# A gated cross-attention and mixture-of-experts kernel on one core: value weights, turns and one GpSimd pass moved, and the last expert's scatter written without adding

## The reference

```python
x = x + tanh(g_xattn) * slot_attention(layernorm(x), ctx)       # x: 4 x 1024 x 256, ctx: 4 x 64 x 256
x = x + tanh(g_ffn) * moe(layernorm(x))

def slot_attention(slots, P):                  # three iterations over the same weights
    k, v = rmsnorm(P) @ Wk.T, rmsnorm(P) @ Wv.T
    for _ in range(3):
        scores = (rmsnorm(slots) @ Wq.T) @ k.T * SCALE
        attn = softmax(scores, axis=-2); attn = attn / (attn.sum(-1) + EPS)
        slots = gru_cell(attn @ v, slots)      # gates from wih (on the update) and whh (on the slots)

def moe(x):                                    # 16 experts, each takes its own 512 best tokens
    score = sigmoid(h @ gate_w.T); topk_score, topk_ids = top_k(score.T, 512)
    eo = silu(xin @ gw.T + gb) * (xin @ up_w.T + up_b)          # xin = h[topk_ids]
    eo = eo @ down_w.T + down_b
    out = zeros.at[topk_ids].add(eo * topk_score)
    return out + shared_ffn(x)
```

## Time and profile before

| | |
|---|---|
| median of 3 runs | 1107.53 us (1107.29 to 1108.12) |
| profiled execution: its own time | 1108.25 us |
| profiled execution: span from first to last instruction | 1106.5 us |
| mean granted TensorE clock | 0.994 of full |
| busy: PE, PEld, DVE, ACT, POOL | 98%, 84%, 70%, 49%, 31% of the span |

### The profile page before, as it was taken

How to read it: one execution, slowest core, us unless ns; L and a number is a source line. 1 busy time by engine, 2 the same in 40 slices (tenths; PEclk the granted TensorE clock), 3 DMA queues, 4 the chain that set the end, 5 groups by cost and what they waited for, 6 DMA issues and landing times.

```text
span 1106.5 us, 17708 instructions
## 1 busy us (share of the span) xinstructions
PE 1079.6 (98%) x6087; PEld 930.8 (84%) x6087; DVE 778.8 (70%) x1504; ACT 546.2 (49%) x830; POOL 341.7 (31%) x352
## 2 busy tenths in 40 slices
PE   6899999999999999999999999999999999999996
PEld 4687888888888778888888888988889888888896
DVE  7888687878789877787556666566665666656663
ACT  4455545454447843333555554455454544545442
POOL 6123444444205100000214233343333433324332
PEclk9899999999999999999999999999999999999999
DMA  7601010101226441212663443544434445344421
GB/s 247 153 1 34 6 38 1 39 1 39 79 78 192 149 129 20 38 20 40 194 192 94 134 115 119 148 99 130 132 104 147 107 125 144 92 143 123 111 35 20
DMA packets 61323, 105.39 MB, mean 95 GB/s; under 512 B 12128, under 2 KB 50272, under 8 KB 56928
## 3 DMA queue, kind: packets, MB, share of 16 engines
q1 hardware_dynamic: 43904, 82.78, 23.4%
q0 software_dynamic: 16512, 21.50, 12.0%
q10 hardware_dynamic: 864, 0.55, 0.2%
HBM read 74.11 MB, written 21.27 MB: 86 GB/s over the span
## 4 chain that ended last, share of the span: by engine, by line
PE 92%; DVE 5%; issue 1%; DMA 1%; ACT 1%; POOL 0%; SPq 0%; DVEq 0%
PE wide L1313 30%; PE wide L867 16%; PE down L1327 16%; PE wide L1162 8%; PE down L1174 4%; PE down L935 3%; PE wide L874 3%; PE wide L876 3%; PE wide L1359 2%; PE side L1299 1%; PE side L1146 1%; PE side L305 1%; PE side L959 1%; PE down L1373 1%; DVE stats L1896 1%
## 5 line engine op out<-in xcount | busy, mean ns | idle before, releaser
L2310 DVE SCALAR_TENSOR_TENSOR hid<-wide,b_up,silu 128x512 f32<-128x512 f32 x120 | 90.1, 751 | 161.4 <-PE wide L1313 154.9
L1313 PE MATMUL wide<-xt_hi,w_hi 128*128 128x512 f32 x480 | 188.4, 392 | 0.0
L1313 PE MATMUL wide<-xt_lo,w_hi 128*128 128x512 f32 x480 | 187.8, 391 | 0.0
L1313 PE MATMUL wide<-xt_hi,w_lo 128*128 128x512 f32 x480 | 186.9, 389 | 0.0
L838 POOL DMA_INDIRECT out_tokens<-y,idx_out x64 | 111.4, 1741 | 220.1 <-DVE y L2291 175.0
L1690 ACT ACTIVATE silu<-wide,b_gate 128x512 f32<-128x512 f32 x120 | 82.1, 684 | 143.7 <-PE wide L1313 143.7
L1327 PE MATMUL down<-w_hi,hid_hi 128*128 128x256 f32 x480 | 136.5, 284 | 0.0
L1327 PE MATMUL down<-w_lo,hid_hi 128*128 128x256 f32 x480 | 135.7, 283 | 0.0
L1327 PE MATMUL down<-w_hi,hid_lo 128*128 128x256 f32 x480 | 135.7, 283 | 0.0
L1699 ACT ACTIVATE hid_hi<-hid 128x512 fp32r<-128x512 f32 x120 | 76.0, 633 | 100.2 <-DVE hid L2310 100.2
L2261 DVE TENSOR_TENSOR w_lo<-raw,w_hi 128x768 fp32r<-128x768 f32 x128 | 121.4, 949 | 2.5 <-ACT w_hi L1664 2.5
(11 more groups left out here) (329 smaller groups left out, 2266.9 us busy)
## 6 DMA issues: line engine op xcount, KB each, us to landing
raw<-in_w_expert SPq DMA_DIRECT2D x32, 1536.0 KB, 6.8
x_raw<-in_x SPq DMA_DIRECT2D x16, 256.0 KB, 6.8
out_tokens<-slots SPq DMA_DIRECT2D x16, 256.0 KB, 3.8
token_rows<-work SPq DMA_DIRECT2D x8, 512.0 KB, 3.0
out_tokens<-y POOLq DMA_DIRECT2D x8, 512.0 KB, 6.0
attn<-rms_c SPq DMA_DIRECT2D x24, 128.0 KB, 2.3
attn<-expo SPq DMA_DIRECT2D x22, 128.0 KB, 2.3
x_first<-in_x SPq DMA_DIRECT2D x8, 256.0 KB, 3.2
```

What stands on the lines that cost most here:

```text
L1313: last = nc.tensor.matmul(bank[:, f % 2, :], w[f // HALF_F][:, f % HALF_F, (c + k) * P:(c + k + 1) * P], x_[:, k, :], start=(m == 1), stop ...
L2310: nc.vector.scalar_tensor_tensor(hid[:, f % 2, :], eup[:, f % 2, :], b_up[:, bass.ds(e, 1), f:f + 1].rearrange("p a b -> p (a b)"), silu[: ...
```

## The change

1. **Value weights.** Before, TensorE made pieces 0 and 1 ahead of the second pair of turns, piece 2 after the first `spread_rms`, piece 3 after the scores. Now piece 0 alone stays there, piece 1 follows the first `spread_rms`, piece 2 stands ahead of `column_sums(0)`, piece 3 behind it, in the bank of `gate_x`. ScalarE reads them in a new order: `own_weights(0)` comes after piece 1, `exponentials(0)` ahead of pieces 2 and 3, and `own_weights(1)` last.
2. **One GpSimd pass held.** The squares of group 2 in the first iteration also wait for `v_recd` 2, the end of the second `csum_reciprocal`.
3. **Turn order.** `subtract_hi(0)` goes ahead of `turn_slots(4)`, and `turn_slots(5)` ahead of `turn_h(2)`.
4. **Last expert.** GpSimd gathers the 512 output rows into `got` (free by then), once all earlier adds have landed; `last_bias` becomes bias times weight plus the gathered row, in two steps later in the loop (m = 9 and 11 in place of 4 to 7); and the four scatters write without adding.

```diff
@@ small_banks, vw_bank
-            vw_bank = (1, 2, 3, 0)
+            vw_bank = (1, 3, 3, 4)
@@ gpsimd, squares
+                        if run == G + 2:
+                            pool.wait_ge(v_recd, 2)
                         multiply(g)
@@ gpsimd, turn_of(e, more)
+                    if not more:
+                        pool.wait_ge(t_xt, e + 1)
+                        pool.wait_ge(v_wt, e + 1)
+                        pool.wait_ge(p_out, e + 1)
+                        for j in range(BLK):
+                            pool.indirect_dma_start(got[:, j, 0:D], None, out,
+                                                    bass.IndirectOffsetOnAxis(idx_out[:, j:j + 1], 0)).then_inc(g_in_, 16)
                     pool.wait_ge(k_yo, e + 1)
...
+                        if more:
+                            pool.indirect_dma_start(out, bass.IndirectOffsetOnAxis(idx_out[:, j:j + 1], 0), y[:, j, :],
+                                                    None, compute_op=ALU.add).then_inc(g_add, 16)
+                        else:
+                            pool.indirect_dma_start(out, bass.IndirectOffsetOnAxis(idx_out[:, j:j + 1], 0), y[:, j, :],
+                                                    None).then_inc(g_add, 16)
@@ tensor, setup
                 value_weights(0)
-                value_weights(1)
...
                 spread_rms(0, 0)
-                value_weights(2)
-                spread_rms(0, 1)
+                value_weights(1)
                 pe.wait_ge(a_whi, B)
                 pe.wait_ge(p_wlo, B)
-                pe.wait_ge(e_w, 5)
+                pe.wait_ge(e_w, 4)
                 scores(0, 0, (2, 4), True, (0,))
+                spread_rms(0, 1)
                 scores(0, 0, (2, 4), True, (1,))
-                pe.wait_ge(a_rms, 2)
-                value_weights(3)
...
-                pe.wait_ge(e_w, 7)
+                pe.wait_ge(e_w, 5)
+                value_weights(2)
                 column_sums(0)
+                value_weights(3)
                 turn_rec(0)
@@ tensor, last half iteration
                 def turn_and_subtract():
+                    subtract_hi(0)
                     turn_slots(4, (v_x1, 2))
-                    subtract_hi(0)
...
                 gru_unit(LAST, 1, 2, 0, lambda: subtract_hi(1))
+                turn_slots(5, (v_x1, 5))
                 turn_h(2, (a_hlo, 2))
-                turn_slots(5, (v_x1, 5))
@@ vector, last expert
+                        dve.wait_ge(g_in_, 16 * BLK * (E + 1))
-                    nc.vector.tensor_scalar(y[:, j, :], b_down[:, E - 1, :], weight[:, j, :], None, ALU.mult)\
-                        .then_inc(k_out, 1)
+                    nc.vector.scalar_tensor_tensor(y[:, j, :], b_down[:, E - 1, :], weight[:, j, :], got[:, j, 0:D],
+                                                   ALU.mult, ALU.add).then_inc(k_out, 1)
...
-                    if FE - BLK <= m < FE:
-                        last_bias(m - (FE - BLK))
+                    if m == FE + 1:
+                        last_bias(0)
+                        last_bias(1)
+                    if m == FE + LAG + 1:
+                        last_bias(2)
+                        last_bias(3)
```

More of the change, by code:

```diff
@@ L382, in flamingo_kernel @@
             POOL_LOW = ()
-            small_banks = (side[:, 1, :], down[:, 0, :], down[:, 1, :], side[:, 0, :])
-            vw_bank = (1, 2, 3, 0)
+            small_banks = (side[:, 1, :], down[:, 0, :], down[:, 1, :], side[:, 0, :], gate_x)
+            vw_bank = (1, 3, 3, 4)
             def turn_banks(g):
@@ L837, in turn_of @@
                             pool.wait_ge(k_yo, e + 1 + j)
-                        pool.indirect_dma_start(out, bass.IndirectOffsetOnAxis(idx_out[:, j:j + 1], 0), y[:, j, :],
-                                                None, compute_op=ALU.add).then_inc(g_add, 16)
+                        if more:
[4 more added lines that the diff above has]
+                                                    None).then_inc(g_add, 16)
                     pool.wait_ge(g_add, 16 * BLK * (e + 1))
@@ L1551, in _ @@
                 value_weights(0)
-                value_weights(1)
-                copy_rms(0, 0, True)
                 first_high(1)
                 first_high(3)
+                copy_rms(0, 0, True)
                 copy_rms(0, 1, True)
+                value_weights(1)
                 own_weights(0)
+                exponentials(0)
                 value_weights(2)
                 value_weights(3)
-                exponentials(0)
                 own_weights(1)
```

## The result

| | before | after |
|---|---|---|
| median | 1107.70 us (6 runs, 1107.12 to 1108.36) | 1112.13 us (6 runs, 1111.12 to 1113.19) |
| ratio | | 1.0041, 95% interval 1.0029 to 1.0053 |
| profiled execution: own time, span | 1108.25, 1106.5 us | 1112.92, 1111.2 us |

The forecast was -1.3 us. Measured is +4.4, outside the range that was given, and on the other side. A second measurement gave the same (last experiment: 1.0040, 1.0027 to 1.0054).

A forecast was written before the change was run, and what follows sets the result against it. TensorE, busy for all but about 27 us of 1106.5, was taken to bound the kernel. The terms -0.4 - 0.6 + 1.3 - 1.6 = -1.3, set against the median of 1107.53, gave 1106.2 us, range 1104.7 to 1108.9.

The forecast's parts named there:

- What bounds the kernel: Whole kernel: TensorE busy for all but about 27 us; only its work, its idle time or the tail can be shortened.
- The holes are under a microsecond each: TensorE's waits: what each of the four parts can give is the size of a hole, under 1 us.
- Value weights, -0.4 predicted: Setup up to the first attention: earlier turns, gain limited by GpSimd's low part; -0.4 us, bounds -0.9 and +0.7.
- rival B: Wait ahead of turn_slots(5): clock falls in the longer hole, costing 2.0 to 3.0 us; sum +0.7 to +1.7; chance 0.17.
- The same can happen at 47.7: Ahead of the first attention: TensorE arrives earlier and waits longer, so the clock can fall there too; no size given.
- Half of it stays, so TensorE could turn 1.9 us earlier: Second pair of turns: half of the 3.85 us of pieces stays ahead; bank reads limit the gain to about 0.9.
- The held pass: Second attention, near 96 us: squares held until the reciprocal is through free VectorE; -0.6 us, bounds -0.69 and 0.
- Turn order: Turns near 353 to 366 us: turn_h's 0.87 leaves the hole and subtract_hi(0) delays turn_slots(4) by 0.45; +1.3 us.
- Bounds: 0 and +1.3, without the clock: Limits on the cost of the two swapped turns, leaving out any fall of the clock.
- The last expert: Tail: gathers cost nothing, scatters without the sum are shorter and land sooner; -1.6 us, bounds -2.0 and 0.
- Rival A: Moved turns: the order costs nothing, so the sum is -2.6 us, 1104.9; chance 0.15.
- C: Tail: a scatter costs as much without the sum, so the sum is +0.3 us, 1107.8; chance 0.16.

The follow-up runs named there:

- last experiment: The whole changed kernel measured once more against the kernel before, beside its halves on one chip: 1.0040 (1.0027 to 1.0054).
- the first experiment: The kernel before with the new order of the value weights alone: 1.0027 (1.0015 to 1.0039), +3.0 us.
- the fourth experiment: The changed kernel with filler matmuls and transposes in TensorE's two long waits: 1.0008 against the kernel before, 1109.24 us.
- the third experiment: The kernel before with the held GpSimd pass and the new last expert alone: 0.9975 (0.9966 to 0.9985), 1105.04 us.
- the second and the sixth experiment: The kernel before with both swaps of turns alone: 1.0020; the kernel before with only turn_slots(5) ahead of turn_h(2): 1.0011.
- the twelfth experiment: The kernel before with subtract_hi(0) ahead of turn_slots(4) alone: 1.0003 (0.9994 to 1.0012).

## Why the prediction was wrong

**What bounds the kernel** held: every edit came out as idle or slow time of TensorE, or as tail. "The holes are under a microsecond each" was the blind spot. It is the limit of what can be won, not of what can be lost.

**1. Value weights, -0.4 predicted, +3.8 in the trace, +3.0 timed alone.** This part failed, and with it the sum: two of its terms stood at nothing, and a third was read from a row at half clock.
- The transfer. That the second `vw_hi` would share the engines with the attention's data was written down and got no price, in the sum or in the bounds. From ScalarE's issue to the matmul it was 2.39 us before, 3.25 in the first experiment, 3.39 in the changed kernel; with the hold gone, SP's order makes it 2.79 or 3.97. GpSimd's hold, in contrast, was in the sum: it made 0.4 out of the gain of 0.7 to 0.9. In the first experiment `own_weights(1)` ended at 42.26 (42.2 worked out) and the gain at ScalarE's issue was 0.27. In the changed kernel the same step ended at 43.62, since its clock had fallen at the turns (below). The upper bound of +0.7 held only piece 3 at half clock; I bounded a transfer that meets another by nothing.
- The clock behind the longer wait. It was written as half a sentence of rival B ("The same can happen at 47.7") without a price. It is the largest single item: 1.7 us (18.05 for 16.35), gone in the fourth experiment. Before, the spell lay from 40.9 to 47.7, on nine matmuls that were done before the attention came; after, on work that nothing hid.
- "Half of it stays, so TensorE could turn 1.9 us earlier." The 3.85 us of pieces 0 and 1 were taken at half clock, from 20.4 to 23.8 us; the group of eight matmuls in the timeline took 4.05 us there and 2.75 in the third experiment, where the clock was up. And the column sums came 19.3 to 19.5 us after the first turn in the six other traces with the old order. With the new order they come at 19.0 where the clock stays: 0.8 better than the one trace that the prediction had, but only some 0.4 better than the others. In its place stands a wait of 1.97 to 2.43 us (0.67 to 0.92 in the six). Behind it the clock fell in four of the eight traces that have the change's order: the turns then took 2.67 to 3.51 in place of 1.91 to 2.20, and the column sums came at 20.6.

**2. The held pass** was right in mechanism and size: -0.6 predicted, -0.53 in TensorE's wait, the cast at 0.17, the squares meeting `pre` instead.

**3. Turn order** was right to a few hundredths where the clock stayed: +1.3 predicted, 1.32 measured; the first swap 0.49 for 0.45. (The wait of 2.8 should have been 2.67 by the same rows: 0.60 + 1.06 + 0.56 + 0.45.) What failed is "Bounds: 0 and +1.3, without the clock": the forecast left the clock out because in the earlier trace rows it stayed at 1.00 with 2.37 us of matmuls in the stretch, 1.3 of them besides the turn. The new order takes that turn, 1.06 us of work, out of the hole. Rival B had the place and the sign; its price, 2.0 to 3.0, was near the 1.7 to 2.8 of the traces, its chance of 0.17 too small: the clock fell in four of the five traces with the second swap and no fillers. B's condition, a clock that is down before the slots come, held in the second and the sixth experiment (0.50 from 364.0 and 364.7, slots at 365.0). The changed kernel shows a variant: the first turn still took 1.31, the spell began 0.7 us behind the end of the wait. The Trainium skill (TensorE: Matmul & The Clock Gate, section HAM oscillation) warns that a wait between bursts of matmuls drops the clock. The wait of 4.66 us is of the kind that it describes, and the clock was 0.50 behind it; the waits that it describes are longer than those of 1.97 and 2.64 us, behind which the traces show the same. So the page alone does not give B its place.

**4. The last expert** was right: -1.6 predicted, -1.6 in the trace. The gathers cost nothing, GpSimd's instruction went from 1.54 to 0.97, and from the start of the last one to the end it is 5.6 us in place of 6.7. When it lands (2.8 after its start, by the prediction) no row of the changed kernel says. The Trainium skill (DMA: Bandwidth & Descriptors, section Anatomy of one DMA) would have kept the whole of what follows the instruction, -1.2 for the part. The trace decides otherwise: besides the instruction the data got faster, 0.51 us from the first to the last packet for 1.35, while what follows them to the end grew from 3.2 to 3.5.

Rival A fell (the order does cost), C fell (the plain scatter is cheaper). Not settled: why, with the same issues, ScalarE's first attention DMA is served after SP's third in some executions and before it in others; and how often the clock falls in a given place, for which one profiled execution per kernel is too few. The +4.4 is a difference of medians, its split into parts rests on single traces.

## What to carry to other kernels

A wait that is made longer has two prices, its length and the half clock behind it, and the second falls on work that had been free before; ask of every hole not only how long it is but what work in it keeps the clock up, and what stands behind it. A row of one profiled execution may itself have been taken at half clock: look at the granted clock of the row's own stretch before it becomes a term. And where an edit moves the issue of a transfer or a pass of GpSimd, write down the time at which it meets the next urgent one, since two causes that stand side by side show nothing when only one is removed.

## What was not expected of the hardware

- The same waits, and the clock falls in one execution and not in another: behind 2.66 and 2.70 us ahead of `turn_slots(5)` it stayed at 1.00 in one trace and went to 0.50 in the other. The times spread by some 3 us too (1106.5 to 1109.8 with the turns moved and the value weights as before), but so did those of the kernel before (1106.8 to 1111.0 on the first experiments' chip), so the spread is not shown to come from this place.
- An indirect DMA that adds moves its rows in packets of 1 KB, the plain one in packets of 4 KB (256 against 64 for the last two scatters), at a mean of 144 and 180 ns each.
- GpSimd held VectorE with a pass of 1.85 us even on an instruction of two columns (1.37 us, 0.44 before, and 0.16 with the pass held). The Trainium skill (SBUF — State Buffer, section Who interferes with whom) states that whoever of the two issues first keeps the shared ports for the whole instruction; the traces agree here and at the cast (1.60 before, 0.17 after).
- Two DMAs issued 0.06 us apart by ScalarE and SP were served in either order, 2.4 or 3.3 us from ScalarE's issue to the matmul that waited for it. The Trainium skill (DMA: Bandwidth & Descriptors, section Issuing engines are not separate DMA queues) says that such DMAs interleave on the same engines. Here two issued together ran mostly one behind the other (in the twelfth experiment from 45.54 to 46.30 and from 46.14 to 47.07), and which went first changed from trace to trace.
